# One transformer block on one core: tiles one to four laid out anew, and a new order of ScalarE and VectorE work in the steady step

## The chip, the core and the metric

The kernel runs on one core of a Trainium2 chip. The metric is the device time of one execution in microseconds (us). Engines are called as in the profile: PE (TensorE), DVE (VectorE), ACT (ScalarE), POOL (GpSimd), SP (SyncE, which here only issues DMAs).

## The reference, cut to what matters

A row block `x` of 4096 rows by 1024 goes through a pre-norm attention and a pre-norm dense layer with low-rank experts, both added back:

```python
q = (h @ wq.T + bq).reshape(B, S, H, D)      # h = layernorm(x), H = D = 32
k = (h @ wk.T + bk).reshape(B, S, H, D)
v = (h @ wv.T + bv).reshape(B, S, H, D)
scores = jnp.einsum('bshd,bstd->bsht', q, k) / np.sqrt(D)    # per row: 32 heads against 32 heads
context = jnp.einsum('bsht,bstd->bshd', softmax(scores), v)
x = x + context
y = layernorm(x)
x = x + y @ base_w.T + base_b + SCALING * lora_out           # top 2 of 8 experts, rank 16
```

Attention is inside each row, between its heads, so a tile of 128 rows needs nothing from other rows.

## The kernel before, in words

The rows are cut into T = 32 tiles of 128. Each engine has its own program, written by hand in program order, and engines wait for each other with semaphores alone. Every fp32 factor is split in two fp16 parts, a high part (a cast) and a low part (a subtraction), and a product is made of two or three matmul passes. `first_step()` loads and splits the weights and does tiles 0 and 1; then `step(2)`, a hardware loop over t = 3 to 28, and `step(29)` to `step(31)` follow, and a `tail`. In step t PE does the scores of tile t, the k, q and v projections of tile t+1, the context of tile t between q and v, and the experts and the dense layer of tile t-1.

What the other engines do in step t, by the names that the text uses:

- ACT: `spread` copies the parts of v into the block-diagonal operand `diag` for the context, 16 copies in four groups of four (line 401); `exponentials` (line 922); `probabilities_high` (line 927); `x2_high(t-1)`, the high part of the second layer norm's turned rows, which first come back from a DMA through memory (`fetch_x2`) (line 782); `q_high` (line 910); `low_copy`, the high part of the experts' row (line 830); `v_high` (line 917).
- DVE: `shift` subtracts the row maximum of the scores (lines 1389, 1394); `finish(t-2)` adds the dense result into the output rows and frees its PSUM banks (line 1307); `turn_quads(t+2)` (line 1225) turns the first layer norm's rows; `sum_exponentials` and `probabilities` (lines 1400, 1405, 1407, 1413); `add_bias` takes projections out of PSUM (line 1196); `probabilities_low` (line 1418); `turn_first` (line 1356); `turn_context` (line 1314); the second layer norm, ending in `norm2` (line 1157) and `turn_x2` (line 1247), whose result is parked in memory and fetched; `x1_low` (line 1231).
- POOL: `x2_low(t-1)` (line 604) as soon as `x2_high` is done, `base_bias` (line 645), `row_root`, `root` (line 599) on which `norm2` waits, `second_lo` (line 626) as soon as `q_high` is done, and `v_low` (line 632) as soon as `v_high` is done. `spread` of the next tile waits for `v_low`.
- PE: the second half of the q projection (line 1630) goes to a PSUM bank that `add_bias` of the first half of k must have emptied:

```python
                pe.wait_ge(a_biased, 2 * t + 1)
                project(SECOND, 1, 0, b_acc)
```

The dense layer's last terms (line 1800) wait for `low_copy`. On ACT, `low_copy(t-1)` stands behind `fetch_x2(act, t)`, which waits until the turned rows are parked.

Of the kernel before, what the change touches and what calls it, by code (L numbers as in the profile page):

```python
# [69 lines left out]
def block_kernel(nc, x, wT, agT, lora_b, biases, out):  # L70
    T = x.shape[0] // P
    with ExitStack() as ctx:
# [369 lines left out]
        def _(sp):  # L442
# [94 lines left out]
            for t in range(1, T):  # L537
                if t >= 2:
                    store(t - 2)
                if t + 3 < T:  # L540
                    load_rows(t + 3)
                if t + 1 < T:
                    first_hi(t + 1)
                    first_lo(t + 1)
                if t + 1 < T:
                    load_res(t + 1)
                if t + 3 < T:
                    load_quads(t + 3)
                if t == 1:

                    sp.wait_ge(w_lo_done["base"], KC)
                    load_bias("base")
                if t + 1 < T:
                    park_x2(sp, t, (0, 1))

# [11 lines left out]
        def _(pool):  # L567
# [109 lines left out]
            def step(t):  # L677

                x2_low(t - 1)
                if isinstance(t, int) and t == 2:  # L680
                    base_bias(0)
                if tile(t, 1):
                    base_bias(t - 1)
                if tile(t, 3):
                    row_root(t + 3)
                if tile(t, 1):
                    root(t, var_ready2, rstd_ready2)
                    second_lo(t + 1)
                    if not tile(t, 2):
                        base_bias(t)  # L690
                    v_low(t + 1)
# [8 lines left out]
        def _(act):  # L700
# [173 lines left out]
            def second_step():  # L874

                exponentials(1)
                spread(1, (0, 1))
                copy_quad_stats(3)
                probabilities_high(1)
                spread(1, (2,))  # L880
                k_high(2)
                x2_high(0)
                scale_quads(3)
                high_parts("base", w_hi["base"], 5, 6)
                x1_high(3)
                high_parts("base", w_hi["base"], 6, 7)
                q_high(2)
                row_statistics(4)
                gate_exp(0)
                high_parts("base", w_hi["base"], 7, KC)  # L890
                copy_quad_stats(4)
                low_copy(0)
                scale_quads(4)
                park_x2(act, 1, (2, 3))
                v_high(2)
                fetch_x2(act, 1)
# [53 lines left out]
            def step(t):  # L950
                if not tile(t, 1):
                    return last_step(t)
                if isinstance(t, int) and t == 2:
                    exponentials(t)
                    spread(t, (0,))
                    x2_high(t - 1)
                    spread(t, (1,))
                    probabilities_high(t)
                    spread(t, (2,))
                else:  # L960
                    x2_high(t - 1)
# [10 lines left out]
                q_high(t + 1)  # L972
                park_x2(act, t, (2, 3))
# [15 lines left out]
        def _(dve):  # L989
# [500 lines left out]
            def second_step():  # L1490
# [6 lines left out]
                add_bias(2, 0, FIRST, 0, a_acc, a_biased)  # L1497
                sum_exponentials(1)
                probabilities(1)
                add_bias(2, 1, FIRST, 1, a_acc, a_biased)  # L1500
                turn_first(2)
                spread_v(nc.vector.tensor_copy, NQ - 1)
# [20 lines left out]
                low_low(0)  # L1523
# [3 lines left out]
            def third_step():  # L1527
# [7 lines left out]
                add_bias(3, 1, FIRST, 1, a_acc, a_biased)  # L1535
                spread_v(nc.vector.tensor_copy, NQ - 1)
                probabilities_low(2)
                finish(0, 0)
                finish(0, 1)
                turn_quads(4)  # L1540
                turn_first(3)
                attend_step(2)

            def step(t):
                if isinstance(t, int) and t == 2:
                    return third_step()
                finish(t - 2, 0)
# [4 lines left out]
                if not tile(t, 1):  # L1552
                    return last_step(t)
# [5 lines left out]
                add_bias(t + 1, 1, FIRST, 1, a_acc, a_biased)  # L1559
                probabilities_low(t)  # L1560
# [56 lines left out]
        def _(pe):  # L1617
# [5 lines left out]
            def project(g, n, bank, done):  # L1623
# [11 lines left out]
                with pe.If(any_low[i] > 0):  # L1635
                    for k in range(KC):
                        nc.tensor.matmul(dst, x_hi[:, k, :], w_lo[g][:, k, cols], start=False, stop=False)
                for k in range(KC):
# [196 lines left out]
            def dense_first():  # L1835
# [8 lines left out]
                spread_stats(4)  # L1844
                turn_low(0)
                pe.wait_ge(w_lo_done["base"], KC)
                for n in range(NB):
                    dense(n, KC - 1, KC)

# [215 lines left out]
```

## Time and profile before

| | before |
|---|---|
| median of 3 runs | 1276.71 us (1274.11 to 1278.17) |
| profiled execution, own time | 1278.39 us |
| its span, first to last instruction | 1275.3 us |
| PE busy | 1242.0 us, 97% |
| DVE, ACT, POOL busy | 84%, 58%, 33% |
| mean granted TensorE clock | 0.997 |

The span is the time from the first to the last instruction; the execution's own time is 3.1 us more. A busy share is an average over all stages.

### The profile page before, as it was taken

What the parts mean: (1) busy time and instruction counts of PE and PEld (TensorE: products, weight loads), DVE (VectorE), ACT (ScalarE), POOL (GpSimd) and SP (SyncE); (2) the same over time, 40 slices, a digit from 0 to 9 for tenths busy, and PEclk for the clock granted to TensorE, in tenths of its full rate; (3) what the DMA queues carried; (4) which work ended last, traced back from release to release, by engine and by line L of the source; (5) the groups of instructions that cost most, each with busy time, mean ns of one, the idle gap of its engine ahead of it and who ended that gap; (6) DMA issues with size and microseconds to landing.
All of it is one profiled execution on the core that took longest, in us unless ns stands there. A gap on an engine that the chain in (4) does not pass through costs nothing.

```text
span 1275.3 us, 30571 instructions
## 1 busy us (share of the span) xinstructions
PE 1242.0 (97%) x12314; PEld 642.1 (50%) x12314; DVE 1067.5 (84%) x1492; ACT 743.3 (58%) x1149; POOL 426.5 (33%) x340
## 2 busy tenths in 40 slices
PE   6899989999999999999999999999999999999998
PEld 4554445455554545455454555545455555545454
DVE  5799898888888888888888888888888888888886
ACT  4876646665556666555666655566665556666431
POOL 0113433334423333442333344233334423333320
PEclk9999999999999999999999999999999999999999
DMA  9823543344444334444433444443344444333330
GB/s 367 295 67 85 133 100 92 89 101 115 101 96 97 96 84 101 115 101 97 97 96 84 102 115 101 97 96 96 84 103 115 99 98 96 96 84 87 85 84 33
DMA packets 295447, 136.41 MB, mean 107 GB/s; under 512 B 265072, under 2 KB 266096, under 8 KB 295408
## 3 DMA queue, kind: packets, MB, share of 16 engines
q1 hardware_dynamic: 228688, 112.28, 33.6%
q10 hardware_dynamic: 66720, 23.60, 7.8%
q8 instruction: 26, 0.43, 0.1%
q14 instruction: 13, 0.11, 0.0%
HBM read 86.03 MB, written 33.03 MB: 93 GB/s over the span
## 4 chain that ended last, share of the span: by engine, by line
PE 84%; DVE 7%; DMA 3%; issue 2%; ACT 2%; SPq 1%; POOL 0%; DVEq 0%; ACTq 0%
PE acc L1630 23%; PE dense_acc L1790 23%; PE acc L1639 22%; PE attn_ps L1732 7%; PE dense_acc L1800 2%; DMA work<-wT_dram 2%; PE low_ps L1769 1%; PE low_ps L1762 1%; PE low_ps L1763 1%; PE dense_acc L1805 1%; DMA turn_dram<-x_turned 1%; DVE w_lo_k L1059 1%; ACT work L401 1%; DVE work L1196 1%; DVE work L1157 1%
## 5 line engine op out<-in xcount | busy, mean ns | idle before, releaser
L1790 PE MATMUL dense_acc<-base_parts,x 128*128 128x512 f16 x1488 | 331.2, 380 | 1.1 <-issue 1.0
L401 ACT COPY work<-work 32x512 f16<-32x512 f16 x498 | 306.5, 615 | 12.4 <-PE attn_ps L1732 0.3
L1790 PEld LDWEIGHTS dense_acc<-base_parts,x 128*128 128x128 f16 x1488 | 145.7, 99 | 165.6 <-issue 2.2
L632 POOL TENSOR_TENSOR work<-work 128x1024 f16<-128x1024 f32 x32 | 68.4, 2137 | 225.9 <-ACT work L917 225.9
L1196 DVE SCALAR_TENSOR_TENSOR work<-acc,acc_to_a,biases_sb 128x512 f32<-128x512 f32 x192 | 136.3, 738 | 1.8
L582 POOL TENSOR_TENSOR columns<-columns 128x1 f32<-128x1 f32 x31 | 9.1, 293 | 362.9 <-ACT work L797 362.9
L763 ACT CAST x_hi<-x_turned 128x1024 f16<-128x1024 f32 x31 | 32.4, 1044 | 155.3 <-PE acc L1639 154.4
L1630 PE MATMUL acc<-w_hi_k,x_hi 128*128 128x512 f16 x496 | 117.5, 380 | 1.6 <-issue 1.6
L1630 PE MATMUL acc<-v_parts,x_hi 128*128 128x512 f16 x496 | 117.5, 380 | 0.0
L1639 PE MATMUL acc<-w_hi_k,x_lo 128*128 128x512 f16 x496 | 117.2, 379 | 0.0
L1630 PE MATMUL acc<-w_hi_q,x_hi 128*128 128x512 f16 x496 | 117.2, 379 | 0.0
L1639 PE MATMUL acc<-w_hi_q,x_lo 128*128 128x512 f16 x496 | 117.2, 379 | 0.0
L1639 PE MATMUL acc<-v_parts,x_lo 128*128 128x512 f16 x496 | 117.2, 379 | 0.0
L626 POOL TENSOR_TENSOR work<-work 128x1024 f16<-128x1024 f32 x32 | 97.4, 3044 | 47.5 <-ACT work L910 43.5
L1732 PEld LDWEIGHTS attn_ps<-work 128*32 128x32 f16 x6144 | 86.4, 97 | 30.2 <-issue 26.4
L1732 PE MATMUL attn_ps<-work 128*32 128x128 f16 x6144 | 97.5, 220 | 2.9 <-DVE work L1418 1.7
L1307 DVE SCALAR_TENSOR_TENSOR work<-dense_acc,w_undo_bits,work 128x512 f32<-128x512 f32 x64 | 45.2, 747 | 51.7 <-PE dense_acc L1805 48.2
L825 ACT ACTIVATE columns<-columns 128x1 f32<-128x1 f32 x32 | 6.5, 203 | 135.8 <-issue 92.5
L645 POOL TENSOR_TENSOR work<-work,biases_sb 128x1024 f32<-128x1024 f32 x32 | 75.6, 2363 | 17.6 <-DMA out_dram<-work 15.1
L1314 DVE STREAM_TRANSPOSE work<-attn_ps 128x1024 f32<-128x1024 f32 x32 | 63.2, 1975 | 19.4 <-PE attn_ps L1732 19.3
L1639 PEld LDWEIGHTS acc<-w_hi_k,x_lo 128*128 128x128 f16 x496 | 48.4, 98 | 58.8 <-issue 0.5
L1639 PEld LDWEIGHTS acc<-v_parts,x_lo 128*128 128x128 f16 x496 | 48.5, 98 | 58.6
(217 smaller groups left out, 2070.1 us busy)
## 6 DMA issues: line engine op xcount, KB each, us to landing
work<-x_dram SPq DMA_DIRECT2D x64, 512.0 KB, 3.6
work<-work SPq DMA_DIRECT2D x256, 64.0 KB, 2.0
work<-x_dram SPq DMA_DIRECT2D x124, 128.0 KB, 3.8
out_dram<-work SPq DMA_DIRECT2D x31, 512.0 KB, 2.6
x_turned<-turn_dram ACTq DMA_DIRECT2D x30, 512.0 KB, 3.3
work<-wT_dram SPq DMA_DIRECT2D x16, 512.0 KB, 9.9
turn_dram<-x_turned SPq DMA_DIRECT2D x64, 128.0 KB, 3.9
turn_dram<-x_turned ACTq DMA_DIRECT2D x60, 128.0 KB, 4.4
```

Of the source, the lines that this page charges most:

```text
L401: copy(diag[c * QD:(c + 1) * QD, :, c, j::NQ, :], src).then_inc(vdiag_ready, 1)
L626: nc.gpsimd.tensor_tensor(dense_parts[:, :, 1, :], kq_rows(t), dense_parts[:, :, 0, :], ALU.subtract).then_inc(b_lo_ready, 1)
L632: nc.gpsimd.tensor_tensor(v_parts_t[:, :, 1, :], turned3, v_parts_t[:, :, 0, :], ALU.subtract).then_inc(v_lo_ready, 1)
L645: nc.gpsimd.tensor_tensor(biased, h, bias["base"][:, :], ALU.add).then_inc(x1_biased, 1)
L763: nc.scalar.copy(x_hi[:, :, :], x1_turned).then_inc(xhi_ready, 1)
L1196: nc.vector.scalar_tensor_tensor(out=ev[:, s], in0=acc[bank][:, :], scalar=acc_to_a[:, i:i + 1], in1=bias[g][:, s], op0=ALU.mult, op1=ALU. ...
L1307: nc.vector.scalar_tensor_tensor(out=h[:, s], in0=dense_acc[n][:, :], scalar=w_undo[:, BASE_:BASE_ + 1], in1=h[:, s], op0=ALU.mult, op1=AL ...
L1314: nc.vector.transpose(turned.rearrange("p (h d) -> p d h", h=HEADS), attn_ps[:, :].rearrange("p (t d) -> p d t", t=QD)).then_inc(ctx_turne ...
L1630: nc.tensor.matmul(dst, x_hi[:, k, :], w_hi[g][:, k, cols], start=(k == 0), stop=False)
L1639: mm = nc.tensor.matmul(dst, x_lo[:, k, :], w_hi[g][:, k, cols], start=False, stop=(k == KC - 1))
L1732: mm = nc.tensor.matmul(attn_ps[c * QD:(c + 1) * QD, i4 * P:(i4 + 1) * P], dense_parts[:, i, dense_part, :], diag[:, spread_part, :, i, :] ...
L1790: nc.tensor.matmul(dense_acc[n][:, :], rows_part[:, k, :], w_part[:, k, cols], start=(k == 0 and m == 0), stop=False)
```

## The change

Three things. In tiles 1 and 2 (`second_step`, `third_step`) DVE and ACT work stands in another order: weight splits and the gate ahead of the layer norm's statistics, v copies shared otherwise between ACT and DVE, POOL takes over `x1_low(4)`, SP issues one fetch in place of ACT, and PE's `spread_stats(4)` stands at the end of its dense layer. In every tile PE's first half of k waits for the low part of the rows only ahead of the matmuls that read it. And in the steady step (t = 3 to 30) ACT does six v copies, then `exponentials`, then `x2_high`, and DVE does `shift`, then `finish`, and `turn_quads` behind the two `add_bias` of k. No instruction is added or taken away; 2 v copies of tile 2 go from ACT to DVE.

```diff
@@ pool: step
-                x2_low(t - 1)
                 if isinstance(t, int) and t == 2:
                     base_bias(0)
+                x2_low(t - 1)
...
+                if isinstance(t, int) and t == 2:
+                    x1_low(4)
@@ scalar: step
+                    spread_v(nc.scalar.copy, 2, range(NQ // 2))
+                else:
+                    spread(t, (0,))
+                    spread_v(nc.scalar.copy, 1, range(NQ // 2))
+                    exponentials(t)
+                    x2_high(t - 1)
+                    spread_v(nc.scalar.copy, 1, range(NQ // 2, NQ))
                     spread(t, (2,))
-                else:
-                    x2_high(t - 1)
-                    spread(t, (0,))
-                    exponentials(t)
-                    spread(t, (1, 2))
                     probabilities_high(t)
                     spread(t, (3,))
@@ vector: second_step
                 turn_context(1)
+                base_split(5, 6)
                 turn_quads(3)
-                base_split(5, 6)
                 turn_second(2)
+                base_split(6, 7)
+                gate_top(0)
                 attention_end(1)
-                stats2(1)
-                gate_top(0)
-                base_split(6, 7)
                 gate_rest(0)
                 base_split(7, KC)
+                stats2(1)
+                low_low(0)
                 norm2(1)
@@ vector: step
+                shift(t)
                 finish(t - 2, 0)
                 finish(t - 2, 1)
-                shift(t)
-                if tile(t, 2):
-                    turn_quads(t + 2)
...
                 add_bias(t + 1, 0, FIRST, 0, a_acc, a_biased)
                 add_bias(t + 1, 1, FIRST, 1, a_acc, a_biased)
+                if tile(t, 2):
+                    turn_quads(t + 2)
                 probabilities_low(t)
@@ tensor: keys
                 pe.wait_ge(xhi_ready, t + 1)
-                pe.wait_ge(xlo_ready, t + 1)
...
-                project(FIRST, 0, 0, a_acc)
+                project(FIRST, 0, 0, a_acc, t)
```

On ACT, the start of a steady step (the first step behind the loop is shown, the loop's is the same) before; `CAST x` is `x2_high`, `COPY` are the v copies, `ACTIVATE` is `exponentials`, `CAST work 128x32x32` is `probabilities_high`:

```order
L782 CAST x<-x_turned 128x1024
L401 COPY work<-work 32x2x8x32 x4
L922 ACTIVATE work<-work,columns 128x1024
L401 COPY work<-work 32x2x8x32 x8
L927 CAST work<-work 128x32x32
L401 COPY work<-work 32x2x8x32 x4
L903 CAST work<-work 128x1024
```

and after the change:

```order
L401 COPY work<-work 32x2x8x32 x6
L926 ACTIVATE work<-work,columns 128x1024
L786 CAST x<-x_turned 128x1024
L401 COPY work<-work 32x2x8x32 x6
L931 CAST work<-work 128x32x32
L401 COPY work<-work 32x2x8x32 x4
L907 CAST work<-work 128x1024
```

`exponentials` stands behind six copies where it stood behind four, and `x2_high` directly behind it where it stood ahead of all.

On DVE, the same step before, from `finish` (`dense_acc`) over `shift` (`top`, then `attn_ps,top`), `turn_quads` (`x_turned`), the sum and the probabilities to `probabilities_low`:

```order
L1307 SCALAR_TENSOR_TENSOR work<-dense_acc,w_undo_bits,work 128x512 x2
L1389 TENSOR_REDUCE top<-attn_ps 128x32
L1394 TENSOR_TENSOR work<-attn_ps,top 128x1024
L1225 STREAM_TRANSPOSE x_turned<-work 128x1024
L1400 TENSOR_REDUCE top<-work 128x32
L1405 RECIPROCAL top<-top 128x32
L1407 SCALAR_TENSOR_TENSOR work<-work,top 128x1024
L1413 STREAM_TRANSPOSE work<-work 128x1024
L1196 SCALAR_TENSOR_TENSOR work<-acc,acc_to_a,biases_sb 128x512 x2
L1418 TENSOR_TENSOR work<-work 128x32x32
```

and after the change:

```order
L1403 TENSOR_REDUCE top<-attn_ps 128x32
L1408 TENSOR_TENSOR work<-attn_ps,top 128x1024
L1321 SCALAR_TENSOR_TENSOR work<-dense_acc,w_undo_bits,work 128x512 x2
L1414 TENSOR_REDUCE top<-work 128x32
L1419 RECIPROCAL top<-top 128x32
L1421 SCALAR_TENSOR_TENSOR work<-work,top 128x1024
L1427 STREAM_TRANSPOSE work<-work 128x1024
L1210 SCALAR_TENSOR_TENSOR work<-acc,acc_to_a,biases_sb 128x512 x2
L1239 STREAM_TRANSPOSE x_turned<-work 128x1024
L1432 TENSOR_TENSOR work<-work 128x32x32
```

`finish` moved from ahead of `shift` to behind it, and `turn_quads` from ahead of the sum to between the biases of k and `probabilities_low`.

## Rows read from the trace of the kernel before

**Rows 1.** Busy time by stretch, all engines: from:to, length, then each engine

```profile
160.00:180.00 20.00, 16.76 (x185) 8.81 (x184) 19.73 (x21) 11.84 (x18) 8.90 (x8) 1.00 0.29 84
180.00:200.00 20.00, 17.57 (x164) 8.10 (x162) 15.67 (x27) 7.86 (x14) 6.90 (x4) 0.91 0.56 127
...
1040.00:1080.00 40.00, 40.00 (x383) 20.22 (x382) 33.94 (x48) 22.16 (x35) 16.14 (x11) 1.00 0.43 101
```

**Rows 2.** Timeline of PE, a steady tile: start us, us, engine, line

```profile
976.57 1.52 PE L1732 MATMUL attn_ps<-work 128*32 128x128 f16 x96
...
988.39 1.89 PE L1630 MATMUL acc<-w_hi_q,x_hi 128*128 128x512 f16 x8
...
991.94 1.52 PE L1732 MATMUL attn_ps<-work 128*32 128x128 f16 x96
...
1012.39 1.03 PE L1800 MATMUL dense_acc<-lora_up,low 128*128 128x512 f16 x4
...
1013.78 1.52 PE L1732 MATMUL attn_ps<-work 128*32 128x128 f16 x96
```

**Rows 3.** Timeline of ACT, the same tile

```profile
977.24 1.05 ACT L782 CAST x<-x_turned 128x1024 f16<-128x1024 f32 x1 [1.84 <-DMA x_turned<-turn_dram]
978.20 2.54 ACT L401 COPY work<-work 32x512 f16<-32x512 f16 x4
980.76 1.15 ACT L922 ACTIVATE work<-work,columns 128x1024 f32<-128x1024 f32 x1
...
1011.38 0.27 ACT L830 CAST low<-low_ps 128x128 f16<-128x128 f32 x1 [2.10 <-DMA turn_dram<-x_turned]
```

**Rows 4.** Timeline of DVE, the same tile

```profile
980.62 1.25 DVE L1225 STREAM_TRANSPOSE x_turned<-work 128x1024 f32<-128x1024 f32 x1
981.94 1.22 DVE L1400 TENSOR_REDUCE top<-work 128x32 f32<-128x1024 f32 x1
...
983.59 1.22 DVE L1407 SCALAR_TENSOR_TENSOR work<-work,top 128x1024 f32<-128x1024 f32 x1
...
986.01 1.37 DVE L1196 SCALAR_TENSOR_TENSOR work<-acc,acc_to_a,biases_sb 128x512 f32<-128x512 f32 x2
...
993.52 1.97 DVE L1314 STREAM_TRANSPOSE work<-attn_ps 128x1024 f32<-128x1024 f32 x1 [0.72 <-PE attn_ps L1732]
...
1001.86 0.81 DVE L1157 TENSOR_SCALAR work<-work,mv,columns 128x1024 f32<-128x1024 f32 x1 [0.73 <-POOL columns L599]
1002.59 1.22 DVE L1231 TENSOR_TENSOR x_lo<-x_turned,x_hi 128x1024 f16<-128x1024 f32 x1
```

**Rows 5.** Timeline of POOL, the same tile

```profile
978.36 2.13 POOL L604 TENSOR_TENSOR x<-x_turned,x 128x1024 f16<-128x1024 f32 x1 [0.74 <-ACT x L782]
...
1002.58 3.21 POOL L626 TENSOR_TENSOR work<-work 128x1024 f16<-128x1024 f32 x1 [0.83 <-ACT work L910]
1012.67 2.13 POOL L632 TENSOR_TENSOR work<-work 128x1024 f16<-128x1024 f32 x1 [6.87 <-ACT work L917]
```

**Rows 6.** Timeline of DVE, tile 3

```profile
202.01 2.92 DVE L1407 SCALAR_TENSOR_TENSOR work<-work,top 128x1024 f32<-128x1024 f32 x1
...
206.14 1.37 DVE L1196 SCALAR_TENSOR_TENSOR work<-acc,acc_to_a,biases_sb 128x512 f32<-128x512 f32 x2
...
212.04 1.98 DVE L1314 STREAM_TRANSPOSE work<-attn_ps 128x1024 f32<-128x1024 f32 x1
```

**Rows 7.** Timeline of POOL, tile 3

```profile
201.50 2.35 POOL L645 TENSOR_TENSOR work<-work,biases_sb 128x1024 f32<-128x1024 f32 x1 [2.93 <-DMA out_dram<-work]
```

**Rows 8.** Timeline of PE, tile 3

```profile
206.90 1.90 PE L1630 MATMUL acc<-w_hi_q,x_hi 128*128 128x512 f16 x8
```

**Rows 9.** Timeline of DVE, tile 2

```profile
181.06 2.53 DVE L1157 TENSOR_SCALAR work<-work,mv,columns 128x1024 f32<-128x1024 f32 x1 [0.73 <-POOL columns L599]
```

**Rows 10.** Timeline of POOL, tile 2

```profile
180.40 0.55 POOL L599 TENSOR_TENSOR columns<-columns 128x1 f32<-128x1 f32 x1 [1.96 <-DVE columns L1150]
180.91 2.12 POOL L626 TENSOR_TENSOR work<-work 128x1024 f16<-128x1024 f32 x1
```

More of the change, by code:

```diff
@@ L554, in _ @@
                     park_x2(sp, t, (0, 1))
+                if t == 1:
+                    fetch_x2(sp, 1)
             store(T - 2)
@@ L878, in second_step @@
                 copy_quad_stats(3)
+                spread_v(nc.scalar.copy, 2, range(NQ - 1))
                 probabilities_high(1)
-                spread(1, (2,))
+                spread_v(nc.scalar.copy, 2, range(NQ - 1, NQ))
                 k_high(2)
                 x2_high(0)
+                high_parts("base", w_hi["base"], 5, 6)
                 scale_quads(3)
-                high_parts("base", w_hi["base"], 5, 6)
+                high_parts("base", w_hi["base"], 6, 7)
                 x1_high(3)
-                high_parts("base", w_hi["base"], 6, 7)
                 q_high(2)
+                high_parts("base", w_hi["base"], 7, KC)
+                gate_exp(0)
                 row_statistics(4)
-                gate_exp(0)
-                high_parts("base", w_hi["base"], 7, KC)
+                low_copy(0)
                 copy_quad_stats(4)
-                low_copy(0)
                 scale_quads(4)
@@ L895, in second_step @@
                 v_high(2)
-                fetch_x2(act, 1)
             def k_high(t):
@@ L972, in step @@
                 q_high(t + 1)
+                if isinstance(t, int) and t == 2:
+                    gate_exp(1)
+                    normalise_quads(5)
+                    park_x2(act, 2, (2, 3))
+                    low_copy(1)
+                    v_high(3)
+                    fetch_x2(act, 2)
+                    return
                 park_x2(act, t, (2, 3))
@@ L1497, in second_step @@
                 add_bias(2, 0, FIRST, 0, a_acc, a_biased)
+                add_bias(2, 1, FIRST, 1, a_acc, a_biased)
                 sum_exponentials(1)
                 probabilities(1)
-                add_bias(2, 1, FIRST, 1, a_acc, a_biased)
+                spread_v(nc.vector.tensor_copy, NQ - 1)
                 turn_first(2)
-                spread_v(nc.vector.tensor_copy, NQ - 1)
                 dve.wait_ge(at_ready, 3)
@@ L1535, in third_step @@
                 add_bias(3, 1, FIRST, 1, a_acc, a_biased)
+                spread_v(nc.vector.tensor_copy, 2, range(NQ // 2, NQ))
                 spread_v(nc.vector.tensor_copy, NQ - 1)
                 probabilities_low(2)
+                turn_quads(4)
                 finish(0, 0)
                 finish(0, 1)
-                turn_quads(4)
                 turn_first(3)
-                attend_step(2)
+                dve.wait_ge(at_ready, 4)
+                add_bias(3, 0, SECOND, 2, b_acc, b_biased)
+                add_bias(3, 1, SECOND, 0, b_acc, b_biased)
+                turn_context(2)
+                first_low(3)
+                attention_end(2)
+                turn_second(3)
+                stats2(2)
+                gate_top(1)
+                gate_rest(1)
+                norm2(2)
+                turn_x2(2)
+                dve.wait_ge(bt_ready, 4)
+                add_bias(3, 0, "v", 1, v_acc, v_biased)
+                low_low(1)
+                add_bias(3, 1, "v", 2, v_acc, v_biased)
+                turn_third(3)
             def step(t):
@@ L1546, in step @@
                     return third_step()
+                if not tile(t, 1):
+                    finish(t - 2, 0)
+                    finish(t - 2, 1)
+                    shift(t)
+                    return last_step(t)
+                shift(t)
                 finish(t - 2, 0)
                 finish(t - 2, 1)
-                shift(t)
-                if tile(t, 2):
-                    turn_quads(t + 2)
-                if not tile(t, 1):
-                    return last_step(t)
                 sum_exponentials(t)
@@ L1621, in _, with project @@
             any_low = [None, None]
-            def project(g, n, bank, done):
+            def project(g, n, bank, done, low_tile=None):
                 i = 1 if g == "v" else 0
@@ L1637, in project @@
                         nc.tensor.matmul(dst, x_hi[:, k, :], w_lo[g][:, k, cols], start=False, stop=False)
+                if low_tile is not None:
+                    pe.wait_ge(xlo_ready, low_tile + 1)
                 for k in range(KC):
@@ L1843, in dense_first @@
                     dense(n, KC - 2, KC - 1)
-                spread_stats(4)
                 turn_low(0)
@@ L1848, in dense_first @@
                     dense(n, KC - 1, KC)
+                spread_stats(4)
             def context(p):
```

1 line of the change is left out of this document (removed).

## The prediction

> **What bounds the kernel now.** I read first the busy time by stretch, then PE's timeline, and then the timelines of the other engines over one steady tile, to see how late each of them may be. In the steady part PE is busy for all of 40 us of 40 [rows 1], and one tile takes it 37.21 us, from the scores at 976.57 to those at 1013.78 [rows 2]. So 28 tiles of the change's steady step (t = 3 to 30) run at PE's own pace, and an order of ACT or DVE work can win nothing there. It can only lose, once something that PE waits for comes too late. Time is left only at the start: from 160 to 200 us PE is idle for 3.24 + 2.43 us, and the granted clock of the second half is 0.91, worth 0.09 x 20 = 1.8 us [rows 1].
>
> How late may the others be? I count from the first v copy, at 978.20, and call that moment S [rows 3]. Two places matter. The second half of q starts at 988.39, which is S + 10.19 [rows 2], and needs the first k bias, which DVE starts at 986.01, S + 7.81 [rows 4]. And DVE, ACT, the parking DMA and POOL form a ring that comes back to the next tile's first copy: `turn_context` at 993.52 [rows 4], the second layer norm, parking, `low_copy` at 1011.38 [rows 3], `v_high`, and `v_low`, which ends at 1012.67 + 2.13 = 1014.80 [rows 5]. From `turn_context` to that end are 21.28 us. Here `turn_context` had waited for PE for 0.72 us [rows 4], so the ring has a little to spare, not much.
>
> **The change part by part: the steady step.** ACT's copies take 0.64 us each (2.56 us from the first copy to the exponentials) [rows 3]. Six instead of four put the exponentials at S + 3.84, 1.28 us later. `x2_high` no longer waits for its fetch ahead of the copies, but that wait lay ahead of S and was hidden. `finish` behind `shift` fills DVE's wait for the exponentials and costs nothing there; its old place was an idle one too.
>
> Then two things collide. `x2_high` now follows the exponentials (1.15 us) directly, and POOL's `x2_low` starts 1.12 us after `x2_high` (977.24 to 978.36) [rows 3, 5]: that is the exponentials' start + 2.27. DVE's multiplication by the reciprocal sum, line 1407, starts at 983.59 - 980.76 = 2.83 behind them [rows 3, 4]. So POOL begins 0.56 us ahead of it, every tile. What that does stands in tile 3: there line 1407 started at 202.01 while POOL worked from 201.50 to 203.85, and took 2.92 us instead of 1.22, ending 1.08 us after POOL [rows 4, 6, 7]. With POOL's 2.13 us [rows 5] it now ends at 2.27 + 2.13 + 1.08 = 5.48 behind the exponentials' start instead of 4.05, 1.43 us late.
>
> The first k bias follows at S + 3.84 + (986.01 - 980.76) + 1.43 = S + 10.52 [rows 3, 4]. In tile 3 PE's second half of q started 0.76 us after the bias did (206.14, 206.90), later than its turn by some 0.1 us [rows 6, 8], so that wait is a real one. Now it starts at S + 11.28 instead of S + 10.19: **PE waits about 1.1 us in each tile**, and nothing covers it, since q is next in its order. The context keeps its 3.55 us behind it (988.39 to 991.94) [rows 2] and starts at S + 14.83.
>
> `turn_context`: in tile 3 it came 5.90 us after the first bias with DVE never waiting long (206.14 to 212.04) [rows 6]; `turn_quads` between them adds 1.2 (its row says 1.25 [rows 4], and the next instruction starts a little before the end). That is S + 17.6, against 993.52 - 978.20 = S + 15.32: 2.3 us later.
>
> `norm2` is the second collision. It starts 8.34 us behind `turn_context` (993.52 to 1001.86) [rows 4], so at S + 25.96. POOL's `second_lo` starts 10.64 us behind PE's context (991.94 to 1002.58) [rows 2, 5] if POOL is free: S + 25.47. But POOL is still at `root`, on which `norm2` itself waits, and takes the next instruction 0.15 us before DVE gets going. This is the case of tile 2: `root` at 180.40, `second_lo` at 180.91, `norm2` at 181.06 and 2.53 us long instead of 0.81 [rows 4, 9, 10]. Cost: 1.72 us on the ring. In the steady tiles before, `second_lo` came 0.72 us after `norm2` and so escaped.
>
> The Trainium skill has a rule for this pair (SBUF — State Buffer, section "SBUF: two separate sides"): VectorE, with two SBUF inputs or in a 2-port mode, and GpSimd share a port pair as an exclusive lock, and whichever starts first blocks the other for its whole length. By that rule the second collision is certain as soon as `second_lo` is 0.01 us ahead. A row says less: in the steady tile `second_lo` starts at 1002.58, line 1231 at 1002.59, and line 1231 still takes its plain 1.22 us while POOL takes 3.21 instead of 2.12 [rows 4, 5, 10]; there the DVE instruction before held on. Read so, a lead of 0.15 us might not do, and the sum would be that of the first rival below.
>
> The ring: S + 17.6 + 1.72 + 21.28 = S + 40.6. The next tile's copies cannot start before that, so the period is 40.6 us instead of 37.21, **3.4 us more**, of which 1.1 appear at q and the rest where PE waits for the gate's row and for `low_copy` ahead of line 1800. Over 28 tiles: 95 us; I take off 3 for the last two, which have no rows left to prepare and (tile 30) no `turn_quads`. SP's queue moves too: `store` waits for the later `finish`, and `load_rows` for `turn_quads`, which comes some 9 us later in the tile (from 980.62 [rows 4] to behind the biases), so that its rows land near the moment when ACT's `row_statistics`, itself later, wants them. I cost that at nothing, and at up to 1 us a tile if ACT must wait.
>
> **The start.** The new order of tiles 1 and 2, the later wait for the low rows, the v copies given to DVE and the fetch on SP can at most give back 3.24 + 2.43 + 1.8 = 7.5 us [rows 1]. Against them, `stats2(1)` now stands behind two weight splits and the gate, and PE's `spread_stats(4)` needs POOL's `row_root(4)`, queued behind the root of those statistics; that may cost up to 3 us, an estimate from where these instructions stand. And tile 3 cannot start its copies before `v_low(3)`, which hangs on the fetch and on `low_copy(1)`, hardly moved. Between -3 and +7.5 I take a gain of 2, near the middle.
>
> **The sum.** 1278.39 (own time of the profiled execution) + 95 - 3 - 2 = 1368.4. That execution lies 1.7 us above the median of the runs, so I predict **1367 us**. About 0.3% (3.8 us) is what a measurement of this kernel can tell from no change.
>
> **The rivals.**
> - *One collision only.* `norm2` escapes: ring S + 17.6 + 21.28 = 38.9, 1.7 us more per tile, 47 in all, 1322 us. For it: the lead is 0.15 us, and line 1231 got through at a lead of 0.01. Against it: tile 2, the same lead exactly. It decides at a `second_lo` that starts behind `norm2`.
> - *Both, and the clock falls.* With idle pieces of 1 us and more in each tile, the granted clock may drop as between 180 and 200 us, 1.8 us a time [rows 1]: 28 x 1.8 = 50 more, 1417 us. Against it: from 160 to 180 us there were 3.24 us of idle time at clock 1.00.
> - *No collision matters.* If line 1407 is not held, `turn_context` is at S + 3.84 + 5.25 + 7.1 = S + 16.2 and the ring at 37.5: 0.3 us a tile, 8 in all, 1283 us with the start's gain.
> - *Faster.* The ring stays within PE's 37.21 us and the start gives back 5 of its 7.5 us: 1272 us. This needs line 1407 ahead of `x2_low`, that is, a fetch that comes back more than 2 us after the exponentials' end, and `v_low` no later than now. The rows before have the fetch back ahead of S [rows 3], so I see no reason for it.
>
> **How the numbers follow.** Chances: two collisions 0.58, one 0.18, clock 0.06, none 0.09, faster 0.09. The likeliest case's own range is 1340 to 1395 (0.5 us a tile either way, and SP's possible 1 us). The range reaches down past the single collision: **1300 to 1395**, which leaves out the clock and the two cheap cases. Slower: 0.58 + 0.18 + 0.06 and most of the fourth, 0.88; within 0.3%: 0.04; faster: 0.08.
>
> **What the profile of the changed kernel would show.** Right: line 1421 (old 1407) near 2.8 us in the steady tiles with `x2_low` beginning half a us ahead of it; PE idle about 1.1 us ahead of q's second half, released by DVE's bias; `norm2` near 2.5 us with `second_lo` just ahead; PE idle ahead of line 1800, released by `low_copy`; a period near 40.6 us. Wrong: a period of 37.2, line 1421 at 1.22 us, PE without idle time after tile 3. The prediction fails if `x2_low` starts later than I place it, or if the ring between `turn_context` and `v_low` gets shorter than its 21.28 us.

## The result and the profile after

The changed kernel takes 1364.8 us (median of 4 runs, 1363.8 to 1365.7); the kernel before takes 1277.2 us on the same chip (4 runs, 1274.1 to 1278.2). The ratio is 1.069, with a 95% interval of 1.0675 to 1.0705. I had predicted 1367 us in a range of 1300 to 1395. The profiled execution took 1365.1 us by its own time, with a span of 1363.3 us against 1275.3 before.

The page of the profile shows how little a busy share tells: PE still stands at 92% (97% before). It is the chain of what ended last that tells them apart: PE had 84% of it before and has 7% now, and the rest runs through DVE, POOL, ACT and "issue", time on the chain in which an engine waited for nothing that the profile shows. Busy shares, then the chain by engine:

```profile
PE 1260.3 (92%) x12314; PEld 637.3 (47%) x12314; DVE 1138.2 (83%) x1493; ACT 739.9 (54%) x1147; POOL 419.1 (31%) x341
...
issue 36%; DVE 23%; POOL 15%; ACT 13%; PE 7%; DMA 3%; DVEq 1%; SPq 1%; ACTq 0%; POOLq 0%
```

Busy time by stretch after; the last row answers to the steady row of [rows 1], the first two show where the clock fell at the start:

```profile
140.00:160.00 20.00, 15.56 (x154) 7.40 (x153) 16.39 (x27) 9.48 (x18) 8.60 (x9) 0.91 0.64 143
...
200.00:220.00 20.00, 16.20 (x157) 7.37 (x156) 16.92 (x15) 13.85 (x21) 8.19 (x7) 0.91 0.16 47
1040.00:1080.00 40.00, 37.62 (x369) 18.55 (x367) 33.67 (x43) 21.63 (x35) 12.90 (x10) 1.00 0.36 90
```

A steady tile is one turn of the ring. ACT's timeline, with S, the first v copy, at 1045.76 (answers to [rows 3]; the first row is tile 3):

```profile
197.24 3.82 ACT L401 COPY work<-work 32x512 f16<-32x512 f16 x6 [2.24 <-POOL work L634]
...
1045.76 3.82 ACT L401 COPY work<-work 32x512 f16<-32x512 f16 x6 [2.25 <-POOL work L634]
1049.61 1.15 ACT L926 ACTIVATE work<-work,columns 128x1024 f32<-128x1024 f32 x1
...
1086.24 1.90 ACT L401 COPY work<-work 32x512 f16<-32x512 f16 x3 [2.25 <-POOL work L634]
```

DVE's timeline, the same tile (answers to [rows 4]): the multiplication, the first k bias, `probabilities_low`, `turn_context`, `norm2`:

```profile
1052.43 2.54 DVE L1421 SCALAR_TENSOR_TENSOR work<-work,top 128x1024 f32<-128x1024 f32 x1
...
1056.18 1.37 DVE L1210 SCALAR_TENSOR_TENSOR work<-acc,acc_to_a,biases_sb 128x512 f32<-128x512 f32 x2
...
1058.62 1.18 DVE L1432 TENSOR_TENSOR work<-work 128x1024 f16<-128x1024 f32 x1
...
1063.13 1.98 DVE L1328 STREAM_TRANSPOSE work<-attn_ps 128x1024 f32<-128x1024 f32 x1
...
1071.49 2.54 DVE L1171 TENSOR_SCALAR work<-work,mv,columns 128x1024 f32<-128x1024 f32 x1 [0.73 <-POOL columns L601]
```

POOL's timeline: `x2_low`, `base_bias`, `root`, `second_lo`, `v_low` (answers to [rows 5]):

```profile
1051.77 2.12 POOL L606 TENSOR_TENSOR x<-x_turned,x 128x1024 f16<-128x1024 f32 x1 [6.04 <-ACT x L786]
1053.85 3.34 POOL L647 TENSOR_TENSOR work<-work,biases_sb 128x1024 f32<-128x1024 f32 x1
...
1070.84 0.55 POOL L601 TENSOR_TENSOR columns<-columns 128x1 f32<-128x1 f32 x1 [2.27 <-DVE columns L1164]
1071.35 2.13 POOL L628 TENSOR_TENSOR work<-work 128x1024 f16<-128x1024 f32 x1
1084.07 2.14 POOL L634 TENSOR_TENSOR work<-work 128x1024 f16<-128x1024 f32 x1 [10.59 <-ACT work L921]
```

Two pairs are to be seen. `x2_low` begins 0.66 us ahead of line 1421, which then takes 2.54 us instead of 1.22 and ends at 1054.97, 1.08 us behind `x2_low`. `second_lo` begins 0.14 us ahead of `norm2`, which takes 2.54 us instead of 0.81. The lengths are the same in all of tiles 4 to 28, with leads of 0.65 to 0.67 and of 0.13 to 0.15 us. And the ring closes without slack: `v_low` ends at 1086.21, and the next tile's first copy starts at 1086.24. From S to S are 40.48 us here.

PE's timeline: tile 1, tile 3, and the three places in the steady tile where it waits:

```profile
150.32 0.39 PE L1786 MATMUL attn_ps<-stat_rows,same_row 128*128 128x8 f32 x2 [2.96 <-POOL stat_rows L594]
150.56 1.65 PE L1839 MATMUL dense_acc<-lora_up,low 128*128 128x512 f16 x4
...
208.42 3.21 PE L1666 MATMUL acc<-w_hi_q,x_hi 128*128 128x512 f16 x8 [3.80 <-DVE work L1210]
...
1054.12 1.89 PE L1678 MATMUL acc<-w_hi_q,x_lo 128*128 128x512 f16 x8
1056.95 1.90 PE L1666 MATMUL acc<-w_hi_q,x_hi 128*128 128x512 f16 x8 [0.93 <-DVE work L1210]
...
1080.26 0.33 PE L1820 MATMUL low_ps<-ident,low 128*128 128x128 f32 x1 [1.20 <-DVE low L1307]
...
1083.11 1.04 PE L1839 MATMUL dense_acc<-lora_up,low 128*128 128x512 f16 x4 [0.57 <-ACT low L834]
```

PE's waits over the whole span, by line and what released it: total us, times, longest. The kernel before has none of the three in its steady tiles, and only one wait of 2.4 us for the gate's row, in tile 2:

```profile
PE low_ps L1820 <- DVE low L1307: 31.6, 27, 1.3
PE acc L1666 <- DVE work L1210: 28.9, 28, 3.8
PE dense_acc L1839 <- ACT low L834: 13.9, 26, 0.6
```

Where the 88.0 us of span went follows from the start of `shift`'s first row in each tile (tile 3: 196.57 before, 194.21 after; tile 4: 233.88 and 237.08). The new start wins 2.4 us up to tile 3, and tile 3 alone, at 42.87 instead of 37.31 us, loses 5.6. Tiles 4 to 29 take 40.43 us on average instead of 37.21, which is 26 x 3.22 = 83.7, and tile 30 adds 1.1: -2.4 + 5.6 + 83.7 + 1.1 = 88.0.

### The profile page after: what moved, and what is told of

Same layout as the page of the kernel before. It is cut to its first block, busy times and chain, and to the rows that moved or that the text cites. A ratio compares the mean times of both kernels' runs of the same rounds, so it can differ in the third digit from the quotient of the medians.

```text
span 1363.3 us, 30543 instructions
## 1 busy us (share of the span) xinstructions
PE 1260.3 (92%) x12314; PEld 637.3 (47%) x12314; DVE 1138.2 (83%) x1493; ACT 739.9 (54%) x1147; POOL 419.1 (31%) x341
## 4 chain that ended last, share of the span: by engine, by line
issue 36%; DVE 23%; POOL 15%; ACT 13%; PE 7%; DMA 3%; DVEq 1%; SPq 1%; ACTq 0%; POOLq 0%
ACT work L401 7%; DVE work L1421 5%; POOL work L634 4%; POOL work L628 4%; DVE work L1370 4%; DVE work L1210 3%; POOL columns L586 3%; DVE top L1414 3%; ACT work L926 3%; ACT work L797 2%; DVE work L1432 2%; DMA work<-wT_dram 1%; PE dense_acc L1829 1%; POOL columns L584 1%; POOL columns L601 1%
## 5 line engine op out<-in xcount | busy, mean ns | idle before, releaser
L634 POOL TENSOR_TENSOR work<-work 128x1024 f16<-128x1024 f32 x32 | 68.4, 2138 | 316.9 <-ACT work L921 316.9
L606 POOL TENSOR_TENSOR x<-x_turned,x 128x1024 f16<-128x1024 f32 x31 | 66.3, 2139 | 175.2 <-ACT x L786 175.2
L647 POOL TENSOR_TENSOR work<-work,biases_sb 128x1024 f32<-128x1024 f32 x32 | 103.0, 3219 | 11.4 <-DMA out_dram<-work 9.8
L1403 DVE TENSOR_REDUCE top<-attn_ps 128x32 f32<-128x1024 f32 x32 | 39.1, 1222 | 75.6 <-PE attn_ps L1771 75.6
L584 POOL TENSOR_TENSOR columns<-columns 128x1 f32<-128x1 f32 x31 | 19.0, 612 | 267.7 <-ACT work L801 267.7
L1171 DVE TENSOR_SCALAR work<-work,mv,columns 128x1024 f32<-128x1024 f32 x33 | 74.9, 2269 | 22.4 <-POOL columns L601 22.4
L1666 PEld LDWEIGHTS acc<-w_hi_q,x_hi 128*128 128x128 f16 x496 | 46.4, 98 | 95.0 <-DVE work L1210 42.6
L628 POOL TENSOR_TENSOR work<-work 128x1024 f16<-128x1024 f32 x32 | 69.5, 2173 | 25.3 <-ACT work L914 21.4
```

Source lines behind the costliest of these rows:

```text
L606: nc.gpsimd.tensor_tensor(x2_lo, x2_f32, x2_hi, ALU.subtract).then_inc(x2lo_ready, 1)
L628: nc.gpsimd.tensor_tensor(dense_parts[:, :, 1, :], kq_rows(t), dense_parts[:, :, 0, :], ALU.subtract).then_inc(b_lo_ready, 1)
L634: nc.gpsimd.tensor_tensor(v_parts_t[:, :, 1, :], turned3, v_parts_t[:, :, 0, :], ALU.subtract).then_inc(v_lo_ready, 1)
L647: nc.gpsimd.tensor_tensor(biased, h, bias["base"][:, :], ALU.add).then_inc(x1_biased, 1)
L1171: nc.vector.tensor_scalar(dst, src, mv[:, i, 0:1], rstd2[:, 0:1], ALU.subtract, ALU.mult).then_inc(ready, 1)
L1666: nc.tensor.matmul(dst, x_hi[:, k, :], w_hi[g][:, k, cols], start=(k == 0), stop=False)
```

## The experiments

Two theories stood against each other. **A**, that of the prediction: the steady loss is made by DVE instructions that POOL's hold, in two pairs. **B**: it comes from the new order itself, the later exponentials and `turn_quads` ahead of `turn_context`. Periods are the mean of tiles 4 to 29; "shift(3)" and "shift(4)" are the starts of `shift` in those tiles. Where an interval stands, the time is the median of 4 to 12 executions; e2, e3, e5, e6 and e7 stand on one execution each. The medians of the kernel before beside them lay between 1276.7 and 1277.9 us.

| run | us | ratio, 95% interval | shift(3) | shift(4) | period |
|---|---|---|---|---|---|
| before | 1277.2 | | 196.57 | 233.88 | 37.21 |
| changed | 1364.8 | 1.069, 1.0675 to 1.0705 | 194.21 | 237.08 | 40.43 |
| e1, both orders old | 1280.8 | 1.0028, 1.0016 to 1.0039 | 195.06 | 237.16 | 37.21 |
| e2, x2_high later | 1346.4 | | 195.71 | 237.31 | 39.69 |
| e3, second_lo waits | 1319.9 | | 193.48 | 236.23 | 38.70 |
| e4, both edits | 1297.8 | 1.0159, 1.0144 to 1.0175 | 193.75 | 234.51 | 37.97 |
| e5, steady order alone | 1365.9 | | 196.53 | 237.00 | 40.44 |
| e6, ACT's order old | 1277.5 | | 192.16 | 234.31 | 37.21 |
| e7, DVE's order old | 1444.0 | | 194.07 | 239.81 | 43.30 |
| e8, three edits | 1283.4 | 1.0050, 1.0033 to 1.0066 | 191.62 | 231.99 | 37.40 |
| e9, start, step 3 peeled | 1280.5 | 1.0020, 1.0011 to 1.0029 | 194.78 | 236.39 | 37.21 |
| e10, start, not peeled | 1281.5 | 1.0026, 1.0017 to 1.0036 | 193.17 | 237.55 | 37.21 |
| e11, step 3 anew | 1278.5 | 1.0005, 0.9996 to 1.0013 | 194.35 | 233.76 | 37.21 |
| e12, and two moves on POOL | 1274.1 | 0.9982, 0.9972 to 0.9992 | 191.37 | 229.07 | 37.26 |

**e1: the new start with the old steady order.** The changed kernel, in whose steady step ACT and DVE work as before:

```diff
-  shift(t); finish(t-2, 0..1); sum; probabilities; add_bias k; turn_quads(t+2); probabilities_low
+  finish(t-2, 0..1); shift(t); turn_quads(t+2); sum; probabilities; add_bias k; probabilities_low
-  6 copies; exponentials; x2_high(t-1); 6 copies; probabilities_high; 4 copies
+  x2_high(t-1); 4 copies; exponentials; 8 copies; probabilities_high; 4 copies
```

> The changed kernel with ACT's and DVE's steady order put back as before; tiles 1 and 2 stay new. Theory A (the loss comes only from the steady step, where x2_low and second_lo hold the port that DVE shares with POOL): the period is 37.2 us again and the 2.4 us that tile 3's scores won at the start stay, 1275 us, 1 to 4 us below the kernel before. Rival B (the new tiles 1 and 2 leave the engines in a bad phase that the steady step keeps): period well above 37.5 us and over 1300 us.

The period is back at 37.21 us, but the start's gain is not there: 1280.8 us, where theory A had 1275. Tile 3 takes 42.10 us. DVE's `turn_quads` there waited 4.5 us for POOL's `x2_low` of tile 2, which reads the buffer that `turn_quads` writes:

```profile
202.07 1.25 DVE L1237 STREAM_TRANSPOSE x_turned<-work 128x1024 f32<-128x1024 f32 x1 [4.53 <-POOL x L606]
```

That wait is not the whole cause: in e6, below, `turn_quads` stands later and does not wait, and tile 3 takes 42.15 us.

**e2, e3 and e4: one collision less, the other less, both less.** e2 puts `x2_high` two copies (1.28 us) later; e3 lets POOL's `second_lo` wait for `norm2`; e4 does both.

```diff
@@ scalar: step (e2, e4)
-  exponentials(t); x2_high(t-1); 6 copies
+  exponentials(t); 2 copies; x2_high(t-1); 4 copies
@@ pool: step (e3, e4)
                     root(t, var_ready2, rstd_ready2)
+                    if not isinstance(t, int) or t > 2:
+                        pool.wait_ge(xn2_ready, t + 1)
                     second_lo(t + 1)
```

> The changed kernel with x2_high moved behind the next two v copies, 1.28 us later, so that x2_low starts behind the start of line 1421. Theory A: line 1421 takes 1.22 us again; norm2 and second_lo come within 0.1 us of each other: if POOL is first the period is near 39.2 us and the time near 1330 us, if DVE is first 37.5 us and 1283 us. Rival B (line 1421 is slow because the output store's DMA now runs beside it): line 1421 stays near 2.8 us, period 40.4, 1365 us.

> The changed kernel with one added wait on POOL: second_lo waits until norm2 is done. Theory A: norm2 takes 0.81 us instead of 2.54, the first collision stays, the period falls by 1.72 to 38.7 us, and the time to 1317 us. Rival B (norm2 is slow because of DMA traffic or because it waits for its own inputs): norm2 stays near 2.5 us and the time at 1365 us or above.

> Both edits together: x2_high two copies later, and second_lo behind norm2. Theory A: neither line is held, the ring is 37.3 to 37.5 us and the time 1275 to 1285 us. Rival B: as the changed kernel, 1365 us. Rival C (the later exponentials and turn_quads alone cost the time, whatever POOL does): period above 39 us.

e3 fell where theory A has it: DVE's `norm2` at its plain length, POOL's `second_lo` behind it, and a period shorter by 1.73 us, `norm2`'s own 1.73:

```profile
1036.02 0.81 DVE L1173 TENSOR_SCALAR work<-work,mv,columns 128x1024 f32<-128x1024 f32 x1 [0.74 <-POOL columns L601]
```

```profile
1036.99 2.96 POOL L628 TENSOR_TENSOR work<-work 128x1024 f16<-128x1024 f32 x1 [1.08 <-DVE work L1173]
```

e2 freed the multiplication, but the period fell by 0.74 us only, not by the 1.32 that line 1421 had lost. DVE's timeline of e2 shows why: `probabilities_low` is now the held one, 1.75 us instead of 1.18, so 0.57 of the 1.32 came back:

```profile
1003.20 1.75 DVE L1432 TENSOR_TENSOR work<-work 128x1024 f16<-128x1024 f32 x1
...
1037.96 1.23 DVE L1421 SCALAR_TENSOR_TENSOR work<-work,top 128x1024 f32<-128x1024 f32 x1
```

It is `base_bias` that holds it, which follows `x2_low` on POOL. e4 has the same pair and nothing else, DVE first and then POOL:

```profile
1005.48 1.75 DVE L1434 TENSOR_TENSOR work<-work 128x1024 f16<-128x1024 f32 x1
```

```profile
1003.79 2.36 POOL L647 TENSOR_TENSOR work<-work,biases_sb 128x1024 f32<-128x1024 f32 x1
```

e2 came out above what theory A had for it (39.69 us a tile and 1346.4 us, against 39.2 and 1330), and e4 missed its expectation of 1275 to 1285 us, both by a third collision, one that the cure of the first had made.

**e8: the third one too.** e4, and POOL's `base_bias` waits for `probabilities_low`:

```diff
+                    if not isinstance(t, int) or t > 2:
+                        pool.wait_ge(p_lo_ready, t + 1)
                     base_bias(t - 1)
```

> The changed kernel with three edits: x2_high two copies later, second_lo behind norm2, and base_bias behind probabilities_low, which it held for 0.5 us in the run with the first two edits. Theory A (three collisions make the whole steady loss): probabilities_low back at its plain time, no wait of PE for low_copy above 0.2 us, period 37.2 to 37.4 us, 1279 to 1287 us. Rival B (the rest of 0.75 us a tile comes from the order itself, turn_quads ahead of turn_context): period still 37.9, 1297 us.

`probabilities_low` (line 1436) takes 1.18 us again, at 1029.06, and the period falls by 0.57 to 37.40 us. So without a collision 3.03 of the 3.22 us a tile are gone. The changed kernel itself has two, whose lengths add up to the same, 1.32 + 1.73 = 3.05; the third came with the cure. Rival B keeps 0.19: with the multiplication, `probabilities_low` and `norm2` at their plain lengths, `turn_context` still comes 0.7 us later than before (S + 16.05 against S + 15.32), and the ring had 0.6 us to spare (`v_low` ended at 1014.80 and the next copy started at 1015.41). It takes both moves for that, the exponentials 1.28 us later and `turn_quads` ahead of `turn_context`: in e6, with `turn_quads` alone, `turn_context` still waits 0.56 us for PE.

**e5: the steady order alone**, in the kernel before, with its old tiles 1 and 2:

```diff
@@ scalar: step (steady)
+  6 copies; exponentials; x2_high(t-1); 6 copies; probabilities_high; 4 copies
@@ vector: step (steady)
+  shift; finish; sum; probabilities; add_bias k; turn_quads; probabilities_low
```

> The kernel before with the steady order of ACT and DVE alone (t = 3 to 30); tiles 1 and 2, the fetch on SP and the later wait for the low rows are left as before. Theory A (all of the loss is made in the steady step, by DVE instructions held behind POOL's): period 40.4 us from tile 4 on, the multiplication at 2.54 us, norm2 at 2.54 us, 27 tiles x 3.2 = 87 us more, and no start gain to give back: about 1277 + 87 + 0 to 3 = 1364 to 1367 us. Rival B (the new start is what puts x2_high so near to the exponentials, by its later parking): period 37.2 and about 1280 us.

1365.9 us and 40.44 us a tile: the steady order makes all of the loss, whatever the start. Tile 3 takes 40.47 us with the old start and 42.87 with the new one, and tile 4 begins at the same time, 237.00 and 237.08: the new start's 2.4 us are simply waited out.

**e6 and e7: which engine's order?** The changed kernel, e6 with ACT's steady order as before, e7 with DVE's (the lists of e1, one each).

> The changed kernel with ACT's steady order as before (x2_high first, four copies, exponentials), DVE's as changed. Theory A: x2_low works ahead of the exponentials' end and the multiplication takes 1.22 us; it stands before the shifted finish, but the biases come at their old time; norm2 comes with turn_context and is later by turn_quads' 1.2 us at most, so the second collision may or may not stay. Without it: 37.2 us a tile and 1281 us, as with both orders undone. With it (norm2 2.5 us long): ring of 37.2 - 0.7 + 1.2 + 1.7 = 39.4 us a tile, 1277 + 27 x 2.2 = 1336 us. Rival B (the DVE order alone makes the loss): 40.4 us a tile, 1365 us.

> The changed kernel with DVE's steady order as before (finish, shift, turn_quads, sum), ACT's as changed. Theory A: x2_low still starts ahead of the multiplication, which takes 2.5 us, unless turn_quads and the later exponentials move it; the first k bias is late by 2.6 us and PE's second half of q waits about 1.1 us in each tile; norm2 comes earlier than in the changed kernel by turn_quads' 1.2 us and stands ahead of second_lo, 0.81 us long. Period 38.3 us, 1277 + 27 x 1.1 = 1307 us. Rival B (ACT's order alone makes the loss, both collisions): 40.4 us a tile, 1365 us. Rival C (no collision with DVE's old order): 37.2, 1281 us.

e6 is as fast as the kernel before, so far as one execution tells (those of the kernel before range over 3 us). DVE's new order makes none of the steady loss by itself (37.21 us a tile): with `x2_high` first, `x2_low` is over before the multiplication, and in POOL's timeline `second_lo` stands 0.71 us behind `norm2`, which took 0.81 us at 1039.52:

```profile
1040.23 3.22 POOL L628 TENSOR_TENSOR work<-work 128x1024 f16<-128x1024 f32 x1 [0.82 <-ACT work L914]
```

e7 missed in all three theories: 1444.0 us, 43.30 a tile. DVE's timeline of e7 shows a wait that none of my sums had:

```profile
1027.45 1.25 DVE L1239 STREAM_TRANSPOSE x_turned<-work 128x1024 f32<-128x1024 f32 x1 [5.84 <-POOL x L606]
```

`turn_quads` writes the buffer that `x2_low` reads. With `x2_high` behind the exponentials, `x2_low` ends at 1027.31, and in its old place, ahead of the sum, `turn_quads` waits for that with the whole softmax behind it. So the two moves of the change belong together: the late `x2_high` needs the late `turn_quads`. PE then waits 3.87 us in each tile, and its clock falls, as PE's timeline shows by the length of equal groups (1.90 and 1.89 us at full clock):

```profile
1033.41 2.55 PE L1663 MATMUL acc<-w_hi_q,x_hi 128*128 128x512 f16 x8 [3.87 <-DVE work L1210]
1035.75 2.98 PE L1675 MATMUL acc<-w_hi_q,x_lo 128*128 128x512 f16 x8
```

That is 1.7 us in this tile on top of the wait, and on average about 2.2 (43.30 - 37.21 - 3.87): the clock rival of the prediction, at a place where it had not looked.

**e9 and e10: the start by other means.** The kernel before with the later wait for the low rows and, in tile 2, the gate and the low copy ahead of `norm2`; e9 also has step 3 peeled out of the loop, with `x2_high` behind eight copies and `turn_quads` behind `probabilities_low`.

```diff
@@ scalar: step, t == 2 (e9, e10)
+  gate_exp(1); copy_quad_stats(5); park_x2(2); low_copy(1); scale_quads(5); v_high(3); fetch_x2(2)
@@ vector: step, t == 2 (e9, e10)
+  gate_top(1); gate_rest(1)          # ahead of norm2(2)
@@ scalar: step, t == 3 (e9)
+  4 copies; exponentials; 4 copies; x2_high(2); 4 copies; probabilities_high; 4 copies
```

> Not the changed kernel but the one before with what the runs so far speak for: the later wait for the low rows, in tile 2 the gate and the low copy ahead of norm2, and step 3 peeled out of the loop with x2_high behind eight copies and turn_quads behind probabilities_low; the steady order is as before. Theory A (the start can give back part of its 7.5 us if tile 3 does not take it away again): shift(3) 2 to 4 us earlier than 196.6 and a period of tile 3 below 39 us: 1272 to 1275 us, ratio 0.996 to 0.999. Rival B (tile 3 gives it back, as with the steady order undone): 1277 to 1281 us.

> As the run with step 3 peeled, but without the peel: the later wait for the low rows and, in tile 2, the gate and the low copy ahead of norm2. Theory A: v_low(3) comes earlier because low_copy(1) does, tile 3 starts 1 to 2 us earlier and keeps it: 1274 to 1277 us. Rival B: no change that can be measured, or the norm of tile 2, now later, makes tile 3 wait: 1277 to 1281 us.

Both have the lost start of rival B (e10's 1281.5 us lie just above its range). Tile 3 starts 1.8 and 3.4 us earlier than before and takes 41.61 and 44.38 us. In ACT's timeline of e9 the copies still wait for `v_low`, and the exponentials stand behind them:

```profile
196.16 2.54 ACT L401 COPY work<-work 32x512 f16<-32x512 f16 x4 [2.24 <-POOL work L633]
```

In e10 and e6 it is another late input at the head of the same queue: there `x2_high` stands ahead of the copies and waits for its fetch, in e10 6.96 us, in e6 2.91, while `v_low` ends at 194.51 and 195.43. ACT's timeline of e6:

```profile
196.13 1.04 ACT L786 CAST x<-x_turned 128x1024 f16<-128x1024 f32 x1 [2.91 <-DMA x_turned<-turn_dram]
```

**e11 and e12: step 3 built for that.** The changed kernel with ACT's old steady order; step 3 is peeled, and in it the exponentials stand ahead of all copies, and DVE does the last four. e12 adds two moves on POOL: `second_lo(4)` behind `norm2(3)`, and `row_root(4)` ahead of `root(1)`.

```diff
@@ scalar: step, t == 3 (e11, e12)
+  exponentials; 2 copies; x2_high(2); 6 copies; probabilities_high; 4 copies
@@ vector: step, t == 3 (e11, e12)
   add_bias k; turn_quads(5)
+  4 copies
   probabilities_low(3)
@@ pool: first_step (e12)
-                root(1, var_ready2, rstd_ready2)
                 row_root(4)
+                root(1, var_ready2, rstd_ready2)
@@ pool: step (e12)
+                    if isinstance(t, int) and t == 3:
+                        pool.wait_ge(xn2_ready, t + 1)
                     second_lo(t + 1)
```

> The changed kernel with ACT's steady order as before, and step 3 peeled out of the loop: there the exponentials stand ahead of the v copies (so they no longer wait for v_low), x2_high behind two copies, and DVE does the last four v copies. In the runs with that steady order tile 3 took 42.1 to 42.2 us, since the exponentials stood behind copies that wait for v_low. Theory A (that wait is where the start's gain went): PE's 3 us wait for the first k bias in tile 3 goes, tile 3 takes 37.2 to 39 us, the scores of tile 4 are taken 3 to 5 us earlier than in the kernel before (at 229.5 to 231), and the steady 37.21 us keep that: 1272 to 1275 us, ratio 0.996 to 0.998. Rival B (something else late in tile 3, the context's copies or norm2 held by second_lo, takes the gain): tile 3 at 41 to 42 us and 1277 to 1280 us.

> As the run before it (old steady order on ACT, step 3 peeled, exponentials ahead of the copies there), with two moves on POOL: in tile 3 second_lo behind norm2, which it held for 1.72 us, and in tile 1 row_root(4) ahead of root(1), so that PE does not wait 3.0 us for spread_stats(4). Theory A (these two are what takes the start's gain): norm2 of tile 3 at 0.81 us, no wait for the gate's row in tile 3, tile 3 at 37.6 us instead of 39.4 and tile 1 at 38 to 40 us instead of 41.5: shift of tile 4 at 228 to 231, 1273 to 1276 us, ratio 0.996 to 0.999. Rival B (DVE, which works without a break in tiles 1 and 2, bounds the start): shift of tile 3 unmoved at 192 to 194, only norm2's 1.8 us is won, 1276 to 1278 us.

What e11's expectation says of the runs with the old steady order, that the exponentials waited for `v_low`, holds for them only in part, as e6 has just shown; its edit takes the exponentials ahead of both late inputs. PE's wait for the first k bias is gone in e11, and tile 3 takes 39.41 us. The time missed theory A all the same (1278.5 us against 1272 to 1275): as soon as DVE came earlier it ran into `second_lo` (POOL at 219.17, 0.14 us ahead), here in DVE's timeline:

```profile
219.31 2.53 DVE L1180 TENSOR_SCALAR work<-work,mv,columns 128x1024 f32<-128x1024 f32 x1 [0.73 <-POOL columns L602]
```

In e12 it is free, in DVE's timeline, and `spread_stats(4)` no longer holds PE:

```profile
216.33 0.81 DVE L1182 TENSOR_SCALAR work<-work,mv,columns 128x1024 f32<-128x1024 f32 x1 [0.73 <-POOL columns L602]
```

Tile 4 starts at 229.07, 4.8 us earlier than before. It takes 38.48 us and so gives back 1.3, at two of the three places from above: by starts PE comes 0.56 us late at the gate's row and 0.65 at `low_copy`. 1274.1 us, inside theory A's 1273 to 1276, and 0.9982 of the kernel before: it beats both, by less than the 0.3% that this text calls no change, though the interval excludes 1.

## Why the prediction was right, point by point

**The two collisions.** Both are there in each of tiles 4 to 28, at leads of 0.66 us (I had 0.56) and 0.14 us (0.15), and e3, e4 and e8 show that they cause the loss. A lead of 0.14 us is enough, so the rival of one collision (1322 us) fell. I had left that open between a row and the Trainium skill's rule (SBUF — State Buffer, "SBUF: two separate sides", an exclusive lock for whichever starts first); the trace agrees with the rule. The row with its lead of 0.01 us [rows 4, 5] does not speak against it: `norm2` was at work until 1002.67 (1001.86 + 0.81), and line 1231 followed it directly.

**The terms of the ring** (mine, measured): first k bias S + 10.52, 10.42; context S + 14.83, 14.74; `turn_context` S + 17.6, 17.37; `norm2`'s loss 1.72, 1.73; from `turn_context` to `v_low`'s end, without that loss, 21.28, 23.08 - 1.73 = 21.35. Period 40.6, on average 40.43. What was off is the first collision, 1.32 instead of 1.43 us, since `x2_low` starts 2.16 us behind the exponentials' start and not 2.27, and the way from the first k bias to `turn_context`, 6.95 us instead of 7.1. My sum was 95 - 3 - 2 = 90 us; the span grew by 88.0.

**Where PE waits.** I had 1.1 us at q and "the rest" at the gate's row and ahead of the dense layer's last terms. By starts: line 1666 comes 1056.95 - 1054.12 = 2.83 us behind the group ahead of it instead of 1.73, 1.10 us late. For the other two, e6 has the undisturbed distances in PE's timeline:

```profile
1039.58 8.58 PE L1827 MATMUL dense_acc<-base_parts,x 128*128 128x512 f16 x39
1047.99 0.27 PE L1818 MATMUL low_ps<-ident,low 128*128 128x128 f32 x1
1048.10 2.10 PE L1827 MATMUL dense_acc<-base_parts,x 128*128 128x512 f16 x9
1050.04 1.03 PE L1837 MATMUL dense_acc<-lora_up,low 128*128 128x512 f16 x4
```

8.41 and 1.94 us; after the change 9.77 (from 1070.49) and 2.68 (from 1080.43), so 1.36 and 0.74 more. 1.10 + 1.36 + 0.74 = 3.20 of the 3.27 us by which this tile (40.48) is longer than 37.21.

**The start: a step that failed, too small to show in the time.** I took a gain of 2 us that would last. It was there at tile 3 (2.4 us), and tile 3 took it back, as e5 shows (tile 4 at 237.00 without the new start, at 237.08 with it). What failed is the term of 2 us in the sum: it measured 0. The reason stood in my own sentence that tile 3 cannot start its copies before `v_low(3)`, which I did not carry into the sum, where it cancels the gain, because the exponentials stand behind those copies. `v_low(3)` ends at 197.21, against 196.68 in e5 with the old start, and the first copy follows at 197.24 and 196.70. The 3 us that I allowed for `spread_stats(4)` were right (2.96), and the clock fell behind it (0.91 from 140 to 160 us), which I had not counted. For the last two tiles I had taken 3 us off; it was 1.9 (tile 29 lost 3.4 us and tile 30 1.1, together 4.5 instead of twice 3.22). And 28 tiles cost 90 us and not 95, at 3.22 us and not 3.4. The errors have different signs and add up to 2 us; that 1367 us stood so near to 1364.8 is in part luck.

**What the prediction did not see, without harm here:** that `turn_quads` has to move with `x2_high` (e7), and that `base_bias` waits behind `x2_low` with a third collision (e2, e4). SP's possible 1 us a tile did not come: the ring's terms leave no room for it.

**The clock rival** fell: PE's pauses of 0.57 to 1.20 us left the steady stretch at clock 1.00.

## What to carry to other kernels

When an instruction of DVE or POOL is moved, lay the two timelines side by side and look at every pair of elementwise instructions on SBUF tensors that come within a few us of each other; who starts first, here by 0.14 us, decided 1.7 us on the other, and curing one pair moved another one into its place (e2, e4). Before counting a gain at the start of a pipeline, follow it into the first steady tile: there ACT's queue waited for one late input, and only taking the exponentials ahead of it let a gain through (e11, e12). Two edits can be worth +166 (e7) and 0 us (e6) apart and +88 together, all with the new start and against the kernel before, when one of them spares the other a wait for a buffer: try each alone before judging the pair.

## What the runs showed of the hardware

- An instruction that is held shows its wait in its own length: the multiplication ends 1.08 us behind `x2_low` in the changed kernel at 1054.97, and `norm2` 0.55 us behind `second_lo` at 1074.03, against plain lengths of 1.22 and 0.81 us.
- Not every DVE instruction is held. In e4 `base_bias` worked from 1003.79 to 1006.15; the k bias (from PSUM, 1.37 us at 1003.04) and `turn_quads` (a transpose, 1.24 us at 1004.33) kept their plain lengths beside it, `probabilities_low` (two SBUF inputs) did not.
- When POOL's next instruction has its inputs ready, it has a head start of 0.14 us over the DVE instruction that POOL's last one releases: `root` starts at 1070.84, `second_lo` at 1071.35 and `norm2` at 1071.49. That is how `second_lo` got ahead of `norm2` in tiles 4 to 28.
- Pauses of PE of 0.57 to 1.20 us in the tile shown left the granted clock at 1.00, its level of 2.4 GHz; after pauses of 2.96 us (tile 1) and 3.80 us (tile 3) the 20 us around them had 0.91, and in e7, with 3.87 us, the matmuls behind the pause shown took up to 2.98 us instead of 1.89. The length of a pause alone does not decide it: in tile 2 of the kernel before, PE paused 2.43 us and its next nine matmuls took 3.44 us; in e5, at the same place, it paused 2.44 us and they took 2.11. In e1 a pause of 3.49 us in tile 3 left the 20 us around it at 1.00.
